# Tridiagonalisation on one core: fewer semaphore waits on the vector engine, and b·u moved behind the mixed row

## The chip, the cores and the metric

The kernel runs on one core of a Trainium2 chip. A core has five engines that each follow an instruction stream of their own: PE (TensorE, matmuls), DVE (VectorE), ACT (ScalarE), POOL (GpSimd) and SP (which only issues transfers here). They share the on-chip memories SBUF and PSUM and meet through semaphores: an instruction can add to one when it completes, and an instruction can be held until one has reached a value. The metric is the device time of one execution in microseconds (us); lower is better.

## The reference

The program computes four graph layers on x of 128 x 64 nodes x 256 features. Only the first part of layer 0 matters here: the eigenvectors of a 64 x 64 matrix that is made from the adjacency.

```python
def _L0_gnn_ref(features, A, W1, b1, W2, b2):
    deg = jnp.sum(A, axis=0) + jnp.sum(A, axis=1) - jnp.diagonal(A)
    d_inv_sqrt = jnp.where(deg > 0, jax.lax.rsqrt(deg), 0.0)
    L = jnp.diag(deg) - A
    L_norm = d_inv_sqrt[:, None] * L * d_inv_sqrt[None, :]
    _, U = jnp.linalg.eigh(L_norm)
    agg = jnp.einsum('mn,bnd->bmd', U.T, features)
    h = jax.nn.relu(agg @ W1 + b1)
    out = h @ W2 + b2
    return jnp.einsum('nm,bmd->bnd', U, out)
...
x = _layernorm(x + _L0_gnn_ref(x, adj, ...), axis=-1)
# layer 1: graph convolutions and LSTMs; layer 2: two wide products with batch norms; layer 3: attention
```

Every later product needs U, so the eigenvector work comes first and nothing of the layers runs beside it.

## The kernel before

`tridiagonalise` turns the symmetric 64 x 64 matrix `sym` into a tridiagonal one by 62 Householder steps (`STEPS = NODES - 2`), and collects the reflections in `qT`. Later stages cut the tridiagonal matrix into leaves, sweep them, merge them, and only then start the layers. Each stage is a block that all engines leave together.

One step i works on row i of the matrix, held on all 64 partitions as `rows[i % 2]`, from column e = i + 1 on. Values of one number per partition are columns of small tensors, `col("name", i)`. On DVE a step is a hand-written sequence, and the order of the calls in the loop at L287 is the order on the engine. The trace shows 28 DVE rows a step; they are, by line number of the kernel before:

- L220, L230, L231, L243: from the norm that ACT made (L339) the sign, its reciprocal and then m, the scale of the reflection. `then_inc(m_ready)` on L243 tells ACT.
- L247, L248, L250, L253: the row's head is corrected, the reciprocals `inv_m` and `inv_head` are taken, and b is made from `inv_m` and from `tail2`, a sum of squares that ACT made (L340).
- L259, L265, L267, L269: the product u·y (two rows in the trace, the second reads the accumulator), then beta, `b_y` (b times the PSUM row `y`, for row i + 1) and `b_beta`.
- L271: `b_u`, from `u_col`, which ACT makes (L350) once m is known. ACT's own line L334 and L183 read it.
- L278, L281: `mixed`, a row from `own` (PSUM), `no_tail` (ACT, L346) and `b_y`, and then `factor`.
- L194, L188: `pu`, and then the next row, which needs `factor` and `mixed`.
- L206, L183, L210, L200, L202, L225, L214, L235: the update of `sym` with the step's two rank-one terms, the next row's norm (L200) and its column (L214).

Beside it PE makes four products a step from `sym`: `y` and `own` (L370, L373) as soon as L235 has written `sym`, `p` and `p_col` (L376, L378) once `u_col` is there, and a fifth for `qT` (L363). ACT makes the norm, `tail2`, `turned` (L334), `no_tail` and `u_col`, in this order. POOL subtracts `turned` from `qT` (L391).

What orders the work on one engine is also written out. DVE instructions that read what an earlier DVE instruction wrote wait for a semaphore of DVE's own. `mark` notes at which count of the current semaphore `chain[0]` a result will be there, and `after(...)` waits for the highest count of the results named. Every eighth step `chain[0]` becomes another semaphore, and at that place DVE waits until the old one has reached its last count. The waits for other engines are `dve.wait_ge(p_ready, i + 1)` and the like. Where more than one wait stands ahead of an instruction, all have to be met before it starts.

Of the kernel before, what the change touches and what calls it, by code (L numbers as in the profile page):

```python
# [121 lines left out]
def tridiagonalise(nc, ctx, t, sym, qT, ps, diag, sub, sup, load):  # L122
# [34 lines left out]
    def col(name, i):  # L157
        return wide[name][:, i:i + 1]

    with nc.Block() as block:  # L160
        @block.vector
        def _(dve):
# [5 lines left out]
            def mark(*made):  # L168


                count[made] = done.n + 1
                return done.one()

            def after(*made):


                dve.wait_ge(chain[0], max(count[m] for m in made))

            def minus_update(i):
                e = i + 1  # L180
                dve.wait_ge(p_ready, i + 1)
                dve.wait_ge(b_u_ready, i + 1)
                stt(minus_S[:, e:], p[i % 2][:, e:], col("b_u", i), sym[:, e:], ALU.mult,  # L183
                    ALU.subtract).then_inc(chain[0], mark("minus_S", i))
# [6 lines left out]
            def pu(i):  # L191
                dve.wait_ge(p_ready, i + 1)
                after(("uy", i))
                stt(col("pu", i), p[i % 2][:, i + 1:i + 2], col("m", i), col("uy", i), ALU.mult,  # L194
                    ALU.add).then_inc(chain[0], mark("pu", i))
# [21 lines left out]
            def signed2(i):  # L217
                dve.wait_ge(norm2_ready, i + 1)
                after(("half_sign", i))
                tt(col("signed2", i), col("norm2", i), col("half_sign", i),  # L220
                   ALU.mult).then_inc(chain[0], mark("signed2", i))
# [15 lines left out]

            def scalars(i):


                head = rows[i % 2][:, i + 1:i + 2]
                after(("signed2", i), ("inv", i), ("signed", i))
                stt(col("m", i), col("signed2", i), col("inv", i), col("signed", i), ALU.mult,  # L243
                    ALU.add).then_inc(m_ready, 1)
                dve.wait_ge(m_ready, i + 1)
                dve.wait_ge(r_col_ready, i + 1)
                tt(head, col("m", i), head, ALU.add).then_inc(chain[0], mark("head", i))  # L247
                dve.reciprocal(col("inv_m", i), col("m", i)).then_inc(chain[0], mark("inv_m", i))  # L248
                after(("head", i))
                dve.reciprocal(col("inv_head", i), head).then_inc(chain[0], mark("inv_head", i))  # L250
                dve.wait_ge(tail2_ready, i + 1)
                after(("inv_m", i))
                stt(col("b", i), col("tail2", i), 0.0, col("inv_m", i), ALU.is_gt,  # L253
                    ALU.mult).then_inc(chain[0], mark("b", i))

            def uy(i):
                r, e = rows[i % 2], i + 1
                dve.wait_ge(y_ready, i + 1)
                ttr(junk[2][:, e:], y[i % 2][:, e:], r[:, e:], 1.0, 0.0, ALU.mult, ALU.add,  # L259
                    col("uy", i)).then_inc(chain[0], mark("uy", i))  # L260

            def betas(i):
                e = i + 1
                after(("b", i), ("inv_head", i))
                tt(col("beta", i), col("b", i), col("inv_head", i), ALU.mult).then_inc(chain[0], mark("beta", i))  # L265
                if e < STEPS:
                    ts(b_y[:, e + 1:], y[i % 2][:, e + 1:], col("b", i), None, ALU.mult).then_inc(chain[0], mark("b_y", i))  # L267
                after(("beta", i))
                tt(col("b_beta", i), col("b", i), col("beta", i), ALU.mult).then_inc(chain[0], mark("b_beta", i))  # L269
                dve.wait_ge(u_ready, i + 1)  # L270
                tt(col("b_u", i), col("u_col", i), col("beta", i), ALU.mult).then_inc(b_u_ready, 1)  # L271

            def mix(i):
                e = i + 1
                dve.wait_ge(own_ready, i + 1)
                dve.wait_ge(no_tail_ready, i + 1)
                after(("b_y", i))
                stt(mixed[:, e + 1:], own[i % 2][:, e + 1:], col("no_tail", i), b_y[:, e + 1:], ALU.mult,  # L278
                    ALU.subtract).then_inc(chain[0], mark("mixed", i))
                after(("uy", i), ("b_beta", i))  # L280
                tt(col("factor", i), col("uy", i), col("b_beta", i), ALU.mult).then_inc(chain[0], mark("factor", i))  # L281
# [5 lines left out]
            for i in range(STEPS):  # L287
# [12 lines left out]
                signed(i)  # L300
                scalars(i)
                uy(i)
                betas(i)
                if i + 1 < STEPS:
                    mix(i)
# [5 lines left out]
            last = STEPS - 1  # L311
            b_pu(last)
# [12 lines left out]
        def _(act):  # L325
# [10 lines left out]
            for i in range(STEPS):  # L336
# [7 lines left out]
                if i + 1 < STEPS:  # L344
                    act.wait_ge(tail2_ready, i + 1)
                    act.activation(col("no_tail", i), col("tail2", i), ACT.Relu, bias=1.0,  # L346
                                   scale=-3e38).then_inc(no_tail_ready, 1)
                act.wait_ge(m_ready, i + 1)
                act.wait_ge(r_col_ready, i + 1)
# [2864 lines left out]
```

## Time and profile before

| | us |
|---|---|
| three runs: lowest, median, highest | 2143.3, 2143.85, 2145.32 |
| the profiled execution: its own time | 2142.91 |
| the profiled execution: first to last instruction (span) | 2141.1 |
| of the span: the tridiagonalisation, from its first y product to its last update | 20.2 to 213.4 |
| of the span: leaves, sweeps and merges | 213.4 to about 450 |
| of the span: the layers | about 450 to 2141.1 |

A row of the time line gives the start, the duration, the engine, the line and the operation. DVE overlaps one instruction with the next: the next one may start before the one ahead has ended, so durations add up to more than the time that passes, and what counts is the distance from start to start. Rows with a shape of 64x1 work on one number per partition. Instructions that only wait aren't among the rows.

### The profile page before, as it was taken

The page shows a single profiled execution, that of the slowest core. Times are in us where ns is not written, and L with a number is a line of the kernel's source. Part 1 is how long each engine was busy: PE and PEld are TensorE (multiplying, and loading weights), DVE is VectorE, ACT ScalarE, POOL GpSimd, SP SyncE. Part 2 cuts the span into 40 slices and gives each one's busy share as a digit, 9 for nine tenths or more (in the row PEclk, how much of TensorE's full clock was granted, in tenths as well). Part 3 has the DMA queues.
Part 4 walks back from the last instruction along what each step waited for, and adds up shares of the span by engine and source line. Part 5 has one row for each costly group of instructions (what it writes and reads, how often), then busy time and mean ns, then how long its engine had stood idle before and what let it go on. Part 6 is the DMA issues. An engine that isn't in the chain of part 4 may idle for free.

```text
span 2141.1 us, 32310 instructions
## 1 busy us (share of the span) xinstructions
PE 1787.1 (83%) x9764; PEld 1536.2 (72%) x9764; DVE 1441.6 (67%) x5778; ACT 857.2 (40%) x1766; POOL 661.5 (31%) x1058
## 2 busy tenths in 40 slices
PE   3455333324999999999999999999999999989998
PEld 2333333313999788888889999988888888768886
DVE  7999999986777556544444444444444677877886
ACT  2333122211443466333333333323323465756664
POOL 0011344412234367432333323333332111651221
PEclk9999766656999999999999999999999999999999
DMA  6000000000111000000000000000010311320111
GB/s 192 2 1 2 1 1 1 1 1 20 60 40 40 30 15 15 15 5 10 10 11 10 10 0 10 20 1 0 0 39 10 148 60 60 101 69 21 40 41 60
DMA packets 44705, 62.72 MB, mean 29 GB/s; under 512 B 13985, under 2 KB 33313, under 8 KB 44449
## 3 DMA queue, kind: packets, MB, share of 16 engines
q1 hardware_dynamic: 43984, 61.08, 8.4%
q8 instruction: 51, 0.84, 0.2%
q14 instruction: 78, 0.63, 0.1%
q10 hardware_dynamic: 592, 0.17, 0.0%
HBM read 36.08 MB, written 25.17 MB: 29 GB/s over the span
## 4 chain that ended last, share of the span: by engine, by line
PE 67%; DVE 5%; ACT 3%; POOL 1%; issue 1%; ACTq 0%; another core or an unknown queue 0%; DVEq 0%; POOLq 0%
PE ps L2164 43%; PE ps L2553 4%; PE ps L2755 2%; PE ps L1688 2%; PE ps L1713 2%; PE ps L2769 2%; PE ps L1674 1%; PE ps L1698 1%; PE ps L2809 1%; PE ps L2803 1%; ACT l_raw L1585 1%; PE ps L1665 1%; DVE j_lnstats L1571 1%; PE ps L2792 1%; DVE x L1562 1%
## 5 line engine op out<-in xcount | busy, mean ns | idle before, releaser
L2295 ACT ACTIVATE l_gates<-ps,biases 128x512 f32<-128x512 f32 (+1 forms) x504 | 289.3, 636 | 490.3 <-remote 475.8
L2164 PE MATMUL ps<-l_nodes_in,l_even 128*128 128x512 f32 x1392 | 321.3, 390 | 2.6 <-DVE x L1562 1.9
L2164 PEld LDWEIGHTS ps<-l_nodes_in,l_even 128*128 128x128 f32 x1392 | 260.7, 188 | 59.2 <-DVE x L1562 2.7
L2164 PE MATMUL ps<-l_nodes_in,kept 128*128 128x336 f32 (+1 forms) x1280 | 298.0, 350 | 2.0 <-ACT l_gates L2295 1.8
L2396 DVE TENSOR_TENSOR l_gates<-l_gates 128x512 f32<-128x512 f32 (+1 forms) x72 | 50.3, 698 | 343.1 <-ACT l_gates L2295 343.1
L2076 POOL CAST l_nodes_in<-big 128x512 fp32r (+3 forms) x142 | 100.5, 737 | 549.3 <-remote 519.6
L2164 PEld LDWEIGHTS ps<-l_nodes_in,kept 128*128 128x128 f32 x1280 | 229.2, 188 | 27.4 <-issue 4.3
L2164 PE MATMUL ps<-l_state,l_even 128*128 128x512 f32 x960 | 223.3, 392 | 0.0
L2164 PEld LDWEIGHTS ps<-l_state,l_even 128*128 128x128 f32 x960 | 180.3, 188 | 39.8
L2079 POOL TENSOR_TENSOR l_nodes_in<-big,l_nodes_in 128x512 fp32r<-128x512 f32 (+1 forms) x142 | 200.5, 1433 | 5.7
L995 PE MATMUL ps<-w,sw_xT 128*128 128x128 f32 x256 | 58.2, 419 | 133.8 <-ACT sw_xT L859 133.8
L995 PEld LDWEIGHTS ps<-w,sw_xT 128*128 128x128 f32 x256 | 54.3, 323 | 138.7 <-ACT sw_xT L859 138.7
L2394 DVE TENSOR_TENSOR l_cell<-l_gates 128x512 f32<-128x512 f32 (+1 forms) x72 | 56.7, 788 | 104.7 <-ACT l_gates L2295 104.1
L2164 PE MATMUL ps<-l_state,kept 128*128 128x336 f32 x512 | 120.3, 316 | 0.0
L2315 ACT ACTIVATE l_gates<-l_cell 128x512 f32<-128x512 f32 (+1 forms) x144 | 84.0, 583 | 75.5 <-DVE l_cell L2406 70.1
L2164 PE MATMUL ps<-l_nodes_in,l_odd 128*128 128x336 f32 x352 | 110.9, 315 | 0.0
L2253 PE MATMUL ps<-l_state,kept 128*128 128x512 f32 x384 | 96.1, 400 | 4.1 <-DVE l_state L2372 3.9
L2413 DVE TENSOR_TENSOR big<-l_gates 128x512 f32 (+2 forms) x72 | 85.6, 1206 | 18.6 <-ACT l_gates L2315 17.5
L370 PE MATMUL ps<-sym,td_c_r_col 64*64 64x64 f32 x124 | 27.5, 324 | 81.0 <-DVE sym L235 80.2
L2553 PE MATMUL ps<-n_h,kept 128*128 128x512 f32 x384 | 91.3, 401 | 3.5 <-POOL n_h L2608 2.4
L2553 PEld LDWEIGHTS ps<-n_h,kept 128*128 128x128 f32 x384 | 74.0, 193 | 20.7 <-POOL n_h L2608 2.9
L2164 PEld LDWEIGHTS ps<-l_state,kept 128*128 128x128 f32 x512 | 88.1, 189 | 0.0
(581 smaller groups left out, 3889.2 us busy)
## 6 DMA issues: line engine op xcount, KB each, us to landing
x<-in_x SPq DMA_DIRECT2D x4, 2048.0 KB, 16.9
residual<-s_x SPq DMA_DIRECT2D x16, 512.0 KB, 2.6
x<-residual SPq DMA_DIRECT2D x16, 512.0 KB, 5.3
normed<-l_raw SPq DMA_DIRECT2D x16, 512.0 KB, 2.6
x<-normed SPq DMA_DIRECT2D x16, 512.0 KB, 3.2
out<-a_y SPq DMA_DIRECT2D x15, 512.0 KB, 2.9
l_raw<-in_L_gnn_W SPq DMA_DIRECT2D x16, 256.0 KB, 2.7
l_raw<-in_L_gnn_W SPq DMA_DIRECT2D x4, 512.0 KB, 3.6
```

Of the source, the lines that this page charges most:

```text
L995: mm = pe.matmul(XW[:, i * HID0:(i + 1) * HID0], xT[:, k, i * TILE:(i + 1) * TILE], w1[:, k, :], start=k == 0, stop=k == KD - 1)
L1688: mm = pe.matmul(G[:, i, :], agg1[:, part, k, i * TILE:(i + 1) * TILE].bitcast(F32R), w["wg0"][:, w_part, k, :].bitcast(F32R), start=part ...
L2076: return eng.tensor_copy(cut.windows(nodes_in[:, slot, HIGH, k, :]).bitcast(F32R), cut.nodes(k, u, step))
L2079: return eng.tensor_tensor(cut.windows(nodes_in[:, slot, LOW, k, :]).bitcast(F32R), cut.nodes(k, u, step), cut.windows(nodes_in[:, slot, H ...
L2164: return pe.matmul(ps[:, 4 * j + gate, 0:n], weight[w_part][:, at:at + 128].bitcast(F32R), src[:, part, k, 0:n].bitcast(F32R), start=start ...
L2253: mm = pe.matmul(F[:, c, :], w["w1"][:, w_part, at:at + 128].bitcast(F32R), agg[:, g % 2, part, k, :].bitcast(F32R), start=k == 0 and w_pa ...
L2295: act.activation(gates[:, j, gate, 0:n], ps[:, 4 * j + gate, 0:n], ACT.Tanh if gate == G else ACT.Sigmoid, bias=bias[:, gate * KD + j:gate ...
L2315: act.activation(gates[:, j, G, 0:n], cell[:, j, 0:n], ACT.Tanh).then_inc(t_ready[j], 1)
L2394: dve.tensor_tensor(cell[:, j, 0:n], gi, gg, ALU.mult).then_inc(c_ready[j], 1)
L2396: dve.tensor_tensor(gi, gi, gg, ALU.mult).then_inc(input_ready[j], 1)
L2413: return dve.tensor_tensor(cut.nodes(j, u, step), cut.windows(go), cut.windows(gt), ALU.mult)
L2553: mm = pe.matmul(O[g % 2][:, j, :], w["w2"][:, w_part, at:at + 128].bitcast(F32R), h[:, g % 2, part, c, :].bitcast(F32R), start=c == 0 and ...
```

## The change

Seven edits in `tridiagonalise`, on DVE unless said otherwise:

1. Waits are dropped where a wait that remains covers them: `p_ready` and `b_u_ready` ahead of `minus_S`, `uy` ahead of `pu`, `norm2_ready` and (but for step 0) `half_sign` ahead of `signed2`, `r_col_ready` ahead of the head's correction, and `tail2_ready` ahead of b.
2. The wait for `no_tail_ready`, which stood ahead of `mixed`, now stands ahead of `inv_m`. ACT makes `no_tail` after `tail2`, so it also stands for `tail2_ready`.
3. The wait for `own_ready`, which stood ahead of `mixed`, now stands ahead of `b_y`.
4. `b_u` moves from ahead of `mixed` to behind it, so that `factor` comes behind `b_u`.
5. `factor` no longer names `uy` in its wait; it waits for `b_beta`, which comes later on the same engine.
6. On ACT the wait for `r_col_ready` ahead of `u_col` is dropped.
7. In the last step ACT also makes `no_tail` and DVE also makes `factor`, neither of which is read; b·pu of the last step waits for that `factor`.

`uy`, `betas` and `mix` are joined into `scalars` and `mix`; the operations and their operands are the same.

```diff
--- before.py
+++ after.py
@@ -178,8 +178,6 @@
 
             def minus_update(i):
                 e = i + 1
-                dve.wait_ge(p_ready, i + 1)
-                dve.wait_ge(b_u_ready, i + 1)
                 stt(minus_S[:, e:], p[i % 2][:, e:], col("b_u", i), sym[:, e:], ALU.mult,
                     ALU.subtract).then_inc(chain[0], mark("minus_S", i))
 
@@ -190,7 +188,6 @@
 
             def pu(i):
                 dve.wait_ge(p_ready, i + 1)
-                after(("uy", i))
                 stt(col("pu", i), p[i % 2][:, i + 1:i + 2], col("m", i), col("uy", i), ALU.mult,
                     ALU.add).then_inc(chain[0], mark("pu", i))
 
@@ -215,8 +212,8 @@
                     col("r_col", i)).then_inc(r_col_ready, 1)
 
             def signed2(i):
-                dve.wait_ge(norm2_ready, i + 1)
-                after(("half_sign", i))
+                if i == 0:
+                    after(("half_sign", i))
                 tt(col("signed2", i), col("norm2", i), col("half_sign", i),
                    ALU.mult).then_inc(chain[0], mark("signed2", i))
 
@@ -235,49 +232,45 @@
                 stt(sym[:, i + 1:], rows[i % 2][:, i + 1:], col("x", i), minus_S[:, i + 1:], ALU.mult,
                     ALU.subtract).then_inc(s_ready, 1)
 
-            def scalars(i):
-
-
-                head = rows[i % 2][:, i + 1:i + 2]
+            def m(i):
                 after(("signed2", i), ("inv", i), ("signed", i))
                 stt(col("m", i), col("signed2", i), col("inv", i), col("signed", i), ALU.mult,
                     ALU.add).then_inc(m_ready, 1)
+
+            def scalars(i):
+
+
+                r, e = rows[i % 2], i + 1
+                head = r[:, e:e + 1]
                 dve.wait_ge(m_ready, i + 1)
-                dve.wait_ge(r_col_ready, i + 1)
                 tt(head, col("m", i), head, ALU.add).then_inc(chain[0], mark("head", i))
+                dve.wait_ge(no_tail_ready, i + 1)
                 dve.reciprocal(col("inv_m", i), col("m", i)).then_inc(chain[0], mark("inv_m", i))
                 after(("head", i))
                 dve.reciprocal(col("inv_head", i), head).then_inc(chain[0], mark("inv_head", i))
-                dve.wait_ge(tail2_ready, i + 1)
                 after(("inv_m", i))
                 stt(col("b", i), col("tail2", i), 0.0, col("inv_m", i), ALU.is_gt,
                     ALU.mult).then_inc(chain[0], mark("b", i))
-
-            def uy(i):
-                r, e = rows[i % 2], i + 1
                 dve.wait_ge(y_ready, i + 1)
                 ttr(junk[2][:, e:], y[i % 2][:, e:], r[:, e:], 1.0, 0.0, ALU.mult, ALU.add,
                     col("uy", i)).then_inc(chain[0], mark("uy", i))
-
-            def betas(i):
-                e = i + 1
                 after(("b", i), ("inv_head", i))
                 tt(col("beta", i), col("b", i), col("inv_head", i), ALU.mult).then_inc(chain[0], mark("beta", i))
+
+            def mix(i):
+                e = i + 1
                 if e < STEPS:
+                    dve.wait_ge(own_ready, i + 1)
                     ts(b_y[:, e + 1:], y[i % 2][:, e + 1:], col("b", i), None, ALU.mult).then_inc(chain[0], mark("b_y", i))
                 after(("beta", i))
                 tt(col("b_beta", i), col("b", i), col("beta", i), ALU.mult).then_inc(chain[0], mark("b_beta", i))
+                if e < STEPS:
+                    after(("b_y", i))
+                    stt(mixed[:, e + 1:], own[i % 2][:, e + 1:], col("no_tail", i), b_y[:, e + 1:], ALU.mult,
+                        ALU.subtract).then_inc(chain[0], mark("mixed", i))
                 dve.wait_ge(u_ready, i + 1)
                 tt(col("b_u", i), col("u_col", i), col("beta", i), ALU.mult).then_inc(b_u_ready, 1)
-
-            def mix(i):
-                e = i + 1
-                dve.wait_ge(own_ready, i + 1)
-                dve.wait_ge(no_tail_ready, i + 1)
-                after(("b_y", i))
-                stt(mixed[:, e + 1:], own[i % 2][:, e + 1:], col("no_tail", i), b_y[:, e + 1:], ALU.mult,
-                    ALU.subtract).then_inc(chain[0], mark("mixed", i))
-                after(("uy", i), ("b_beta", i))
+                after(("b_beta", i))
                 tt(col("factor", i), col("uy", i), col("b_beta", i), ALU.mult).then_inc(chain[0], mark("factor", i))
 
             dve.wait_ge(first_ready, 1)
@@ -298,17 +291,16 @@
                     update(i - 1)
                 signed2(i)
                 signed(i)
+                m(i)
                 scalars(i)
-                uy(i)
-                betas(i)
-                if i + 1 < STEPS:
-                    mix(i)
+                mix(i)
                 if i % SPAN == 0:
                     dve.wait_ge(chain[0], done.n)
                     chain[0], done.n = chains[i // SPAN], 0
                     count = dict.fromkeys(count, 0)
                 pu(i)
             last = STEPS - 1
+            after(("factor", last))
             b_pu(last)
             minus_update(last)
             b_p(last)
@@ -341,12 +333,10 @@
                                accum_out=col("tail2", i)).then_inc(tail2_ready, 1)
                 if i >= 1:
                     turn(i - 1)
-                if i + 1 < STEPS:
-                    act.wait_ge(tail2_ready, i + 1)
-                    act.activation(col("no_tail", i), col("tail2", i), ACT.Relu, bias=1.0,
-                                   scale=-3e38).then_inc(no_tail_ready, 1)
+                act.wait_ge(tail2_ready, i + 1)
+                act.activation(col("no_tail", i), col("tail2", i), ACT.Relu, bias=1.0,
+                               scale=-3e38).then_inc(no_tail_ready, 1)
                 act.wait_ge(m_ready, i + 1)
-                act.wait_ge(r_col_ready, i + 1)
                 act.activation(col("u_col", i), ident[:, e:e + 1], ACT.Identity, bias=col("r_col", i),
                                scale=col("m", i)).then_inc(u_ready, 1)
             turn(STEPS - 1)
```

At the first place, DVE from m to beta in step 1 (`td_m_ready` is set by m, `td_chain0` is DVE's own semaphore, the second ISA row of a line reads the accumulator), the kernel before has

```order
L243 SCALAR_TENSOR_TENSOR td_c_m<-td_c_signed2,td_c_inv,td_c_signed 64x1 [waits td_chain0]
L247 TENSOR_TENSOR td_row1<-td_c_m,td_row1 64x1 [waits td_r_col_ready,td_m_ready]
L248 RECIPROCAL td_c_inv_m<-td_c_m 64x1
L250 RECIPROCAL td_c_inv_head<-td_row1 64x1 [waits td_chain0]
L253 SCALAR_TENSOR_TENSOR td_c_b<-td_c_tail2,td_c_inv_m 64x1 [waits td_chain0,td_tail2_ready]
L259 ISA td_junk2,td_c_uy<-ps,td_row1 64x62 [waits td_y_ready]
L259 ISA td_c_uy 64x1
L265 TENSOR_TENSOR td_c_beta<-td_c_b,td_c_inv_head 64x1 [waits td_chain0]
```

and the changed kernel, at the same place,

```order
L237 SCALAR_TENSOR_TENSOR td_c_m<-td_c_signed2,td_c_inv,td_c_signed 64x1 [waits td_chain0]
L246 TENSOR_TENSOR td_row1<-td_c_m,td_row1 64x1 [waits td_m_ready]
L248 RECIPROCAL td_c_inv_m<-td_c_m 64x1 [waits td_no_tail_ready]
L250 RECIPROCAL td_c_inv_head<-td_row1 64x1 [waits td_chain0]
L252 SCALAR_TENSOR_TENSOR td_c_b<-td_c_tail2,td_c_inv_m 64x1 [waits td_chain0]
L255 ISA td_junk2,td_c_uy<-ps,td_row1 64x62 [waits td_y_ready]
L255 ISA td_c_uy 64x1
L258 TENSOR_TENSOR td_c_beta<-td_c_b,td_c_inv_head 64x1 [waits td_chain0]
```

Nothing moved here; the second waits of the head and of b are gone, and `inv_m` has one.

At the second place, DVE from `b_y` to the update's first term in step 1, the kernel before has

```order
L267 TENSOR_SCALAR td_b_y<-ps,td_c_b 64x61
L269 TENSOR_TENSOR td_c_b_beta<-td_c_b,td_c_beta 64x1 [waits td_chain0]
L271 TENSOR_TENSOR td_c_b_u<-td_c_u_col,td_c_beta 64x1 [waits td_u_ready]
L278 SCALAR_TENSOR_TENSOR td_mixed<-ps,td_c_no_tail,td_b_y 64x61 [waits td_chain0,td_no_tail_ready,td_own_ready]
L281 TENSOR_TENSOR td_c_factor<-td_c_uy,td_c_b_beta 64x1 [waits td_chain0]
L194 SCALAR_TENSOR_TENSOR td_c_pu<-ps,td_c_m,td_c_uy 64x1 [waits td_chain0,td_p_ready]
L188 SCALAR_TENSOR_TENSOR td_row0<-td_row1,td_c_factor,td_mixed 64x61 [waits td_chain0]
L206 TENSOR_TENSOR td_c_b_pu<-td_c_pu,td_c_beta 64x1 [waits td_chain0]
L183 SCALAR_TENSOR_TENSOR td_minus_S<-ps,td_c_b_u,sym 64x62 [waits td_b_u_ready,td_p_ready]
```

and the changed kernel has

```order
L264 TENSOR_SCALAR td_b_y<-ps,td_c_b 64x61 [waits td_own_ready]
L266 TENSOR_TENSOR td_c_b_beta<-td_c_b,td_c_beta 64x1 [waits td_chain0]
L269 SCALAR_TENSOR_TENSOR td_mixed<-ps,td_c_no_tail,td_b_y 64x61 [waits td_chain0]
L272 TENSOR_TENSOR td_c_b_u<-td_c_u_col,td_c_beta 64x1 [waits td_u_ready]
L274 TENSOR_TENSOR td_c_factor<-td_c_uy,td_c_b_beta 64x1 [waits td_chain0]
L191 SCALAR_TENSOR_TENSOR td_c_pu<-ps,td_c_m,td_c_uy 64x1 [waits td_p_ready]
L186 SCALAR_TENSOR_TENSOR td_row0<-td_row1,td_c_factor,td_mixed 64x61 [waits td_chain0]
L203 TENSOR_TENSOR td_c_b_pu<-td_c_pu,td_c_beta 64x1 [waits td_chain0]
L181 SCALAR_TENSOR_TENSOR td_minus_S<-ps,td_c_b_u,sym 64x62
```

`b_u` has moved behind `mixed`, and of the three waits of `mixed`, the two of `pu` and the two of `minus_S` one, one and none are left. A line with a number that the two kernels share, as L248, need not be the same statement.

## Rows read from the trace of the kernel before

**Rows 1.** The page: 40 slices of the span, DVE's busy share and PE's clock in tenths.

```profile
DVE  7999999986777556544444444444444677877886
...
PEclk9999766656999999999999999999999999999999
```

**Rows 2.** Busy time by stretch; columns: stretch, its length, engines, granted clock, DMA.

```profile
20.20:213.40 193.20, 96.25 (x618) 74.72 (x618) 186.01 (x1726) 68.21 (x373) 19.05 (x62) 1.00 0.19 50
...
450.00:520.00 70.00, 25.50 (x82) 13.75 (x82) 51.85 (x307) 6.77 (x19) 9.22 (x7) 0.57 0.00 1
```

**Rows 3.** The instructions of line 370: durations in ns, first and last start.

```profile
L370 PE MATMUL ps<-sym,td_c_r_col x124: 311/323/367, 20.2 to 211.3; 64*64 64x64 f32 x124
```

**Rows 4.** Time line, DVE from m to `minus_S`.

```profile
110.73 0.34 DVE L243 SCALAR_TENSOR_TENSOR td_c_m<-td_c_signed,td_c_inv 64x1 f32<-64x1 f32 x1
...
111.11 0.15 DVE L247 TENSOR_TENSOR td_row<-td_c_m,td_row 64x1 f32<-64x1 f32 x1
...
111.19 0.15 DVE L248 RECIPROCAL td_c_inv_m<-td_c_m 64x1 f32<-64x1 f32 x1
111.29 0.15 DVE L250 RECIPROCAL td_c_inv_head<-td_row 64x1 f32<-64x1 f32 x1
111.44 0.15 DVE L253 SCALAR_TENSOR_TENSOR td_c_b<-td_c_tail,td_c_inv_m 64x1 f32<-64x1 f32 x1
111.52 0.18 DVE L259 CUSTOM_DVE_ANT_0 td_junk<-ps,td_row 64x35 f32<-64x35 f32 x1
...
111.64 0.15 DVE L265 TENSOR_TENSOR td_c_beta<-td_c_b,td_c_inv_head 64x1 f32<-64x1 f32 x1
111.71 0.24 DVE L267 TENSOR_SCALAR td_b_y<-ps,td_c_b 64x34 f32<-64x34 f32 x1
...
111.87 0.14 DVE L269 TENSOR_TENSOR td_c_b_beta<-td_c_b,td_c_beta 64x1 f32<-64x1 f32 x1
...
111.94 0.14 DVE L271 TENSOR_TENSOR td_c_b_u<-td_c_u_col,td_c_beta 64x1 f32<-64x1 f32 x1
...
112.08 0.24 DVE L278 SCALAR_TENSOR_TENSOR td_mixed<-ps,td_c_no_tail,td_b_y 64x34 f32<-64x34 f32 x1
112.25 0.14 DVE L281 TENSOR_TENSOR td_c_factor<-td_c_uy,td_c_b_beta 64x1 f32<-64x1 f32 x1
112.32 0.20 DVE L194 SCALAR_TENSOR_TENSOR td_c_pu<-ps,td_c_m,td_c_uy 64x1 f32<-64x1 f32 x1
112.44 0.24 DVE L188 SCALAR_TENSOR_TENSOR td_row<-td_row,td_c_factor,td_mixed 64x34 f32<-64x34 f32 x1
112.61 0.14 DVE L206 TENSOR_TENSOR td_c_b_pu<-td_c_pu,td_c_beta 64x1 f32<-64x1 f32 x1
112.68 0.24 DVE L183 SCALAR_TENSOR_TENSOR td_minus_S<-ps,td_c_b_u,sym 64x35 f32<-64x35 f32 x1
```

**Rows 5.** The same time line, what ACT, POOL and PE do beside it.

```profile
110.57 0.19 ACT L346 ACTIVATE td_c_no_tail<-td_c_tail 64x1 f32<-64x1 f32 x1
...
110.64 0.44 PE L370 MATMUL ps<-sym,td_c_r_col 64*64 64x64 f32 x2 [1.28 <-DVE sym L235]
...
110.75 0.31 POOL L391 TENSOR_TENSOR eg_qT<-eg_qT,td_turned 64x64 f32<-64x64 f32 x1 [2.77 <-ACT td_turned L334]
...
110.88 0.42 PE L373 MATMUL ps<-sym,tab 64*64 64x64 f32 x2
...
111.11 0.39 ACT L350 ACTIVATE td_c_u_col<-tab,td_c_r_col,td_c_m 64x1 f32<-64x1 f32 x1 [0.35 <-DVE td_c_m L243]
...
111.55 0.47 PE L376 MATMUL ps<-sym,td_c_u_col 64*64 64x64 f32 x2 [0.25 <-ACT td_c_u_col L350]
```

**Rows 6.** Time line, DVE at the place of a longer pause.

```profile
152.14 0.23 DVE L278 SCALAR_TENSOR_TENSOR td_mixed<-ps,td_c_no_tail,td_b_y 64x21 f32<-64x21 f32 x1
152.52 0.15 DVE L281 TENSOR_TENSOR td_c_factor<-td_c_uy,td_c_b_beta 64x1 f32<-64x1 f32 x1 [0.16 <-DVE td_mixed L278]
```

**Rows 7.** DMA queues, 100 to 212 us: packets, MB, share of 16 engines.

```profile
q14 instruction: 13, 0.11, 0.3%
```

## The prediction

> **What bounds the kernel now.** I read the 40 slices first. DVE stands at 9 tenths from the second slice to the eighth, and every later stage needs the eigenvectors, so the first 450 us are one line of work that DVE sets [rows 1]. By stretches, the tridiagonalisation takes 193.2 us and DVE is busy in 186.0 of them; PE's clock is at its full level there (1.00, of 2.4 GHz), so no clock gain hides in it [rows 2]. The first y product starts at 20.2 us and the 62nd at about 211.3, so a step takes 191.1/61 = 3.13 us [rows 3]. Then I read one step on the time line. What counts is the distance from start to start. Two rules come out of it:
>
> - A plain 64x1 instruction is followed by the next start after 0.07 us: `b_beta` to `b_u`, `factor` to `pu` [rows 4]. Such pairs are bound by nothing but DVE's own pace.
> - An instruction that needs a result of one close ahead starts 0.03 to 0.04 us after that one has *ended*: m ends at 110.73 + 0.34 = 111.07 and the head's correction starts at 111.11; that one ends at 111.26 and `inv_head` starts at 111.29 [rows 4].
>
> Two places break the second rule. b needs `inv_m`, which ends at 111.19 + 0.15 = 111.34 (111.33 with the third digit), but b starts at 111.44, 0.11 after it. `mixed` needs `b_y`, which ends at 111.71 + 0.24 = 111.95, but starts at 112.08, 0.13 after it [rows 4]. These two have a second wait, and the result waited for in it was late. Other instructions with two waits lose nothing: `minus_S` starts 0.07 after b·pu, `pu` 0.07 after `factor`, the head 0.04 after m's end [rows 4]; there the second wait had been met long before. The Trainium skill (Perfetto Trace Analysis, Identifying Dependency Chains) says that such an instruction may get EventSemaphore instructions of their own ahead of it. My reading of the rows goes with it: the extra wait holds the instruction stream, and the waiting instruction is only handed to DVE when it is met, 0.07 to 0.09 us later than it would start if it waited at DVE's door.
>
> **The change, part by part.** All waits left are single ones.
>
> *Second wait of b gone.* b can start at 111.33 + 0.04 = 111.37 and at least 0.07 behind `inv_head` (111.36). It was 111.44. Gain 0.07 us a step. What follows must not be late: the u·y product needs y from PE, which ends at 110.64 + 0.44 = 111.08 [rows 5] against a new start of 111.45, 0.37 to spare. `beta` comes behind that product as before.
>
> *`mixed` ahead of `b_u`.* Count from the start of `b_y` at 0. Before: `b_beta` 0.16, `b_u` 0.23, `mixed` 0.37, `factor` 0.54 [rows 4]. After: `b_beta` 0.16, `mixed` when `b_y` has ended, 0.24 + 0.035 = 0.275 (the 0.07 spacing alone would give 0.23), `b_u` 0.17 behind it, 0.445, `factor` 0.07 behind that, 0.515. Gain 0.025 to 0.03 us. So taking the waits off `mixed` is worth 0.09, and 0.07 of that is paid back by `b_u` standing on the path, where before it stood in the shadow of `b_y`. From `factor` on nothing differs: `pu` 0.07 later, the row 0.12 behind `pu` (`factor` has ended 0.14 after its start; 0.14 + 0.035 is less than 0.19), b·pu, `minus_S`.
>
> *Waits moved.* `no_tail` ends at 110.57 + 0.19 = 110.76 and `inv_m` starts at 111.19, 0.43 to spare; `own` ends at 110.88 + 0.42 = 111.30 and the new `b_y` comes at 111.64, 0.34 to spare; p ends at 111.55 + 0.47 = 112.02 and the new `pu` comes at 112.22, 0.20 to spare; `u_col` ends at 111.50 and the new `b_u` comes at 112.08 [rows 4, 5]. Each cost 0 while its cover lasts. Behind each of them the whole rest of the step is queued, so beyond its cover it would cost its full delay 62 times.
>
> *Other waits dropped* (`minus_S`, `pu`, `signed2`, the head, ACT's `u_col`): 0. The first two start at DVE's pace already, `signed2` stands ahead of m, the head follows m's end by 0.04, and `u_col` starts at 111.11 with the head, 0.04 behind m's end [rows 4, 5]. A gain ahead of m would also be lost: m lasts 0.34 where a later instruction of the same kind, `pu`, lasts 0.20, and it ends at 111.07, when POOL's subtraction ends at 110.75 + 0.31 = 111.06 [rows 4, 5]. What holds it is POOL, whose start comes from ACT, and both move with the step. Those 0.13 us stay.
>
> *Fewer instructions in the stream.* Six places of a step had a second wait. Now and then DVE pauses where nothing is late: `factor` starts 0.38 behind `mixed` instead of 0.17 [rows 6]; the instruction queue made 13 fetches in 112 us there [rows 7]. If a wait of its own is an instruction of its own, a step shrinks from 34 to 28, and about a sixth of these pauses goes. With some ten of them at 0.2 to 0.3 us in the stage (an estimate from the one row that stands here) that is 0.4 us; ends 0, if the pauses stay in number, and 2.5, if they are hidden altogether. I take 0.4.
>
> *Last step.* `factor` and `no_tail` are added once: 0.07 us of DVE, the other beside it.
>
> *Sum.* 62 x 0.07 = 4.3 (4.7 with 0.076), 61 x 0.028 = 1.7, 0.4 for the pauses, -0.1 for the last step: 6.3 to 6.8, say 6.7 us. The stage hands all of it on, as nothing later runs beside it. One term is open: the first layers run at a mean clock of 0.57 from 450 to 520 us [rows 2], and the clock's rise needn't come at the same place of the work; 2 us of PE work at the 1.2 GHz level instead of 2.4 is 1 us. I take 0 and keep ±1.5 us, the lower bound being that the rise stays at the same time while the work is 6.7 us ahead, which would cost half of that, 3.3. The profiled execution took 2142.91 us, 0.94 under the median of 2143.85; from the one I get 2136.2, from the other 2137.1. I predict the median, **2137.0 us**.
>
> **The rivals.** *Waits cost nothing (chance 0.10).* b starts exactly when `inv_head` ends (111.44) and `mixed` when `b_u` has ended (112.08) [rows 4]. So both might be held by the instruction just ahead draining, and not by their waits. Then b gains nothing and `mixed`, behind `b_beta`, would start when that ends, 111.87 + 0.14 = 112.01, 0.07 earlier, which `b_u` behind it pays back. Sum 0: 2143.5 us. Against it: `inv_head` itself starts 0.04 before the reciprocal `inv_m` ahead of it ends, and `factor` starts 0.07 before `mixed` ends [rows 4], so neither kind of instruction has to drain. The Trainium skill (VectorE: DVE Perf Modes, The DRAIN you can't avoid) speaks against the change: it tells of eight chained copies that took the same 13.88 us with a semaphore behind each and with one behind the last, and has op count matter, not semaphores. By that rule the sum here is this rival's, 0. Rows at which a single wait costs 0.04 agree with it; those where a second one stands cost 0.11 to 0.13 and don't.
>
> *PE becomes late (0.05).* The cover of `pu` shrinks from 0.30 to 0.20. Ends of PE are modelled; were p 0.25 later than the row says, 0.05 to 0.10 of each step would be lost again: 6.7 - 62 x 0.08 = 1.7 us gain, 2142 us.
>
> *A moved wait stalls (0.03), slower than before.* `no_tail` now guards `inv_m`, 0.9 us earlier in the step than `mixed`. On ACT it stands behind `turned`, which waits for PE and POOL. Its cover is 0.43 us. If it came 0.43 + 0.11 = 0.54 later than the row shows, the gain would be eaten; each further 0.07 costs 62 x 0.07 = 4.3 us, so 0.61 late is 2148 us. For it speaks only that all of ACT's line stands ahead; against it, that `turned` starts by ACT's own order and not after a wait.
>
> *The pauses vanish (0.07).* Without waits that hold the stream, it runs ahead of DVE and covers them: 2.5 instead of 0.4, and 2135 us, or a little less with a lucky clock.
>
> **How the numbers follow.** The forecast (0.75) has the range 2134.5 to 2139.5, from the terms' ends and the clock. The range that holds 8 in 10 adds the rival with the vanished pauses and part of the clock's worst case: 2133.5 to 2140.5. A measurement of this kernel can tell 0.2%, 4.3 us, from no change. Faster by more than that, under 2139.6: the forecast with little of its tail (0.73) and the vanished pauses (0.07), 0.80. Within it: the free waits, PE, and the forecast's tail, 0.17. Slower: 0.03.
>
> **What would show it.** In the changed profile b (L252) starts 0.03 to 0.04 behind the end of `inv_m` (L248), `mixed` (L269) as much behind the end of `b_y` (L264); from `b_y` to `factor` (L274) 0.515 instead of 0.54; m still lasts 0.34; a step is 0.10 shorter and the stage ends near 206.7 instead of 213.4. I am wrong if b still starts at the end of `inv_head`, if `pu` starts with p's end, or if the stage gives 6 us and the layers take them back.

## The result, and the profile after

Six runs of the changed kernel took 2135.1 to 2137.0 us, median 2136.06, against 2143.82 for six of the kernel before. The ratio is 0.9962 with a 95% interval of 0.9949 to 0.9975: 7.8 us, or 0.4%, faster, and clear of no change. The prediction was 2137.0 in a range of 2133.5 to 2140.5. The time came out right; the way to it did not quite, as the stretches show.

The first view is busy time by stretch, columns as in [rows 2]. First the kernel before, cut at the last update of `sym`, at the end of PE's last product in the sweeps, at the first product of layer 0 and at the first LSTM product:

```profile
213.40:435.60 222.20, 79.70 (x392) 74.07 (x392) 214.29 (x1846) 51.44 (x154) 89.56 (x399) 0.66 0.00 1
435.60:504.80 69.20, 14.65 (x49) 6.86 (x48) 55.03 (x362) 5.99 (x21) 4.06 (x18) 0.52 0.00 1
504.80:726.70 221.90, 210.36 (x1377) 187.88 (x1378) 160.18 (x335) 82.22 (x95) 68.83 (x59) 0.97 0.11 44
726.70:2141.10 1414.40, 1383.68 (x7321) 1190.63 (x7319) 818.50 (x1464) 648.14 (x1123) 478.60 (x514) 0.99 0.09 30
```

Then the changed kernel, cut at the same places of the work; its first line answers to the first of [rows 2]:

```profile
20.20:204.30 184.10, 96.26 (x618) 74.72 (x618) 178.78 (x1728) 68.34 (x374) 19.25 (x62) 1.00 0.20 52
204.30:427.60 223.30, 76.06 (x392) 71.33 (x392) 214.18 (x1843) 51.43 (x154) 89.64 (x398) 0.66 0.00 1
427.60:496.90 69.30, 14.62 (x49) 6.86 (x48) 55.30 (x365) 5.99 (x21) 4.35 (x20) 0.55 0.00 1
496.90:721.10 224.20, 213.20 (x1377) 190.03 (x1378) 160.26 (x335) 82.33 (x95) 68.86 (x59) 0.96 0.11 43
721.10:2134.70 1413.60, 1382.24 (x7321) 1189.39 (x7319) 818.62 (x1464) 648.24 (x1123) 478.68 (x514) 0.99 0.09 30
```

The tridiagonalisation became 9.1 us shorter (193.2 to 184.1), not the 6.7 of my sum. The sweeps took 1.1 us more and the stretch from layer 0 to the LSTMs 2.3 us more, the rest 0.8 less. The span fell by 6.4.

The time line of one step, DVE, answers to [rows 4]:

```profile
104.01 0.34 DVE L237 SCALAR_TENSOR_TENSOR td_c_m<-td_c_signed,td_c_inv 64x1 f32<-64x1 f32 x1
...
104.46 0.15 DVE L248 RECIPROCAL td_c_inv_m<-td_c_m 64x1 f32<-64x1 f32 x1
104.57 0.15 DVE L250 RECIPROCAL td_c_inv_head<-td_row 64x1 f32<-64x1 f32 x1
104.65 0.14 DVE L252 SCALAR_TENSOR_TENSOR td_c_b<-td_c_tail,td_c_inv_m 64x1 f32<-64x1 f32 x1
...
104.90 0.24 DVE L264 TENSOR_SCALAR td_b_y<-ps,td_c_b 64x35 f32<-64x35 f32 x1
105.07 0.14 DVE L266 TENSOR_TENSOR td_c_b_beta<-td_c_b,td_c_beta 64x1 f32<-64x1 f32 x1
...
105.18 0.24 DVE L269 SCALAR_TENSOR_TENSOR td_mixed<-ps,td_c_no_tail,td_b_y 64x35 f32<-64x35 f32 x1
...
105.35 0.14 DVE L272 TENSOR_TENSOR td_c_b_u<-td_c_u_col,td_c_beta 64x1 f32<-64x1 f32 x1
105.42 0.15 DVE L274 TENSOR_TENSOR td_c_factor<-td_c_uy,td_c_b_beta 64x1 f32<-64x1 f32 x1
105.48 0.20 DVE L191 SCALAR_TENSOR_TENSOR td_c_pu<-ps,td_c_m,td_c_uy 64x1 f32<-64x1 f32 x1
```

`inv_m` ends at 104.61 and b starts at 104.65; before, b started 0.11 behind it. `b_y` ends at 105.14 and `mixed` starts at 105.18; before it was 0.13. From the start of `b_y` to that of `factor` it is now 0.51 instead of 0.54. m still lasts 0.34. Over all steps the medians went from 0.111 to 0.041 us from the end of `inv_m` to b, and from 0.538 to 0.508 from the start of `b_y` to `factor`.

POOL beside m, and the instruction queue from 100 to 205 us (against 13 fetches in 112 us in [rows 7]):

```profile
104.02 0.31 POOL L381 TENSOR_TENSOR eg_qT<-eg_qT,td_turned 64x64 f32<-64x64 f32 x1 [2.66 <-ACT td_turned L326]
```

```profile
q14 instruction: 11, 0.09, 0.3%
```

### The profile page after: what moved, and what is told of

The parts are those of the page before. It is cut to its first block, busy times and chain, and to the rows that moved or that the text cites. A ratio compares the mean times of both kernels' runs of the same rounds, so it can differ in the third digit from the quotient of the medians.

```text
span 2134.7 us, 31888 instructions
## 1 busy us (share of the span) xinstructions
PE 1784.8 (84%) x9764; PEld 1534.4 (72%) x9764; DVE 1434.7 (67%) x5779; ACT 857.5 (40%) x1767; POOL 662.2 (31%) x1058
## 4 chain that ended last, share of the span: by engine, by line
PE 67%; DVE 5%; ACT 3%; POOL 1%; issue 1%; ACTq 0%; another core or an unknown queue 0%; DVEq 0%; POOLq 0%
PE ps L2154 43%; PE ps L2543 4%; PE ps L1678 2%; PE ps L1703 2%; PE ps L2759 2%; PE ps L2745 2%; PE ps L1664 1%; PE ps L1688 1%; PE ps L1655 1%; PE ps L2799 1%; PE ps L2793 1%; ACT l_raw L1575 1%; DVE j_lnstats L1561 1%; PE ps L2782 1%; DVE x L1552 1%
## 5 line engine op out<-in xcount | busy, mean ns | idle before, releaser
L2154 PE MATMUL ps<-l_state,l_even 128*128 128x512 f32 x960 | 223.3, 392 | 0.0
```

Of the source, the lines that this page charges most:

```text
L2154: return pe.matmul(ps[:, 4 * j + gate, 0:n], weight[w_part][:, at:at + 128].bitcast(F32R), src[:, part, k, 0:n].bitcast(F32R), start=start ...
```

## The experiments

Each was timed at least five times beside the kernel before, on the same chip, and profiled once. "Last update" is the start of the 62nd update of `sym` in the profiled execution: 213.4 us before, 204.3 changed. A *late second wait* is a wait beside another one on the same instruction, for a result that isn't ready yet when the instruction's turn comes; a *met* one has been fulfilled long before. Late second waits here are those of b and `mixed`. The head's correction also waits for two, and one of them, m, is late, but that costs nothing; the next section shows the difference. A *pause* is a DVE row that starts over 0.07 us later behind the row ahead than it does in the steps around it. Not counted is what every kernel has: where DVE changes its semaphore, every eighth step, `pu` waits for `factor` and starts 0.11 later.

**The changed kernel again (`changed_again`).**

> The changed kernel once more, on the same chip as the next three, as their yardstick. Both theories: the last update of the matrix starts near 204.3 us, the time is near 2136, 7 to 8 us under the kernel before.

Measured: 2135.15 us against 2142.88, ratio 0.9965 (0.9952 to 0.9979), last update 204.3. Its stretch from layer 0 to the LSTMs differs from that of the first profile, with the same program:

```profile
20.20:204.30 184.10, 96.26 (x618) 74.72 (x618) 178.78 (x1728) 68.31 (x374) 19.28 (x62) 1.00 0.20 52
...
497.20:719.50 222.30, 210.80 (x1376) 188.18 (x1377) 160.10 (x335) 82.26 (x95) 68.85 (x59) 0.97 0.11 44
719.50:2134.90 1415.40, 1383.89 (x7321) 1190.71 (x7319) 818.41 (x1464) 648.11 (x1123) 478.69 (x514) 0.99 0.09 30
```

The tridiagonalisation takes 184.1 us again; the later stretch took 224.2 us in one execution and 222.3 in the other, at mean granted clocks of 0.96 and 0.97. So the 2.3 us that the first profile "took back" there are for the most part not the change's doing. The whole didn't end sooner for it: the rest took 1415.4 us here and 1413.6 in the first profile, and the spans are 2134.9 and 2134.7.

**b·u put back ahead of the mixed row (`bu_back`).**

```diff
+                dve.wait_ge(u_ready, i + 1)
+                tt(col("b_u", i), col("u_col", i), col("beta", i), ALU.mult).then_inc(b_u_ready, 1)
                 if e < STEPS:
                     after(("b_y", i))
                     stt(mixed[:, e + 1:], own[i % 2][:, e + 1:], ...
-                dve.wait_ge(u_ready, i + 1)
-                tt(col("b_u", i), col("u_col", i), col("beta", i), ALU.mult).then_inc(b_u_ready, 1)
```

> The changed kernel with b u ahead of the mixed row again, as in the kernel before; all waits stay as changed. My theory: the move itself costs, since b u then fills the 0.11 us in which mixed waits for b_y anyway. From the start of b_y, mixed starts at 0.30 instead of 0.275 and factor at 0.47 instead of 0.515, so 0.04 us a step, 61 steps, 2.5 us: the last update starts near 201.8, the time is 2 to 2.5 us under the changed kernel. Rival (the move is what lets the wait go, or mixed is better early): the last update at 204.3 or later, the time the same or up to 2.5 us longer.

Measured: 2132.71 us, ratio 0.9952 (0.9939 to 0.9966), last update 201.1, 2.4 us under the changed kernel on the same chip. The time line of DVE:

```profile
106.40 0.24 DVE L264 TENSOR_SCALAR td_b_y<-ps,td_c_b 64x34 f32<-64x34 f32 x1
106.56 0.14 DVE L266 TENSOR_TENSOR td_c_b_beta<-td_c_b,td_c_beta 64x1 f32<-64x1 f32 x1
106.63 0.15 DVE L268 TENSOR_TENSOR td_c_b_u<-td_c_u_col,td_c_beta 64x1 f32<-64x1 f32 x1
106.70 0.24 DVE L271 SCALAR_TENSOR_TENSOR td_mixed<-ps,td_c_no_tail,td_b_y 64x34 f32<-64x34 f32 x1
106.86 0.14 DVE L274 TENSOR_TENSOR td_c_factor<-td_c_uy,td_c_b_beta 64x1 f32<-64x1 f32 x1
```

`factor` comes 0.46 behind `b_y` instead of 0.51. `mixed` starts 0.03 later, since `b_u` is ahead of it, but `b_u` no longer costs its 0.07 behind it. The move, one of the two things that the change did, costs 3.1 us of the stage.

**The move alone, with all waits of the kernel before (`order_alone`).**

```diff
-                dve.wait_ge(u_ready, i + 1)
-                tt(col("b_u", i), col("u_col", i), col("beta", i), ALU.mult).then_inc(b_u_ready, 1)
...
                 stt(mixed[:, e + 1:], own[i % 2][:, e + 1:], col("no_tail", i), b_y[:, e + 1:], ALU.mult,
                     ALU.subtract).then_inc(chain[0], mark("mixed", i))
+                dve.wait_ge(u_ready, i + 1)
+                tt(col("b_u", i), col("u_col", i), col("beta", i), ALU.mult).then_inc(b_u_ready, 1)
                 after(("uy", i), ("b_beta", i))
```

> The kernel before with b u behind mixed and all its waits kept. Theory: mixed stays at 0.37 behind b_y, since its late wait for b_y decides, and b u now adds its 0.07 to the path: 61 x 0.07 = 4.2 us longer, last update near 217.6, the time near 2147. Rival (mixed is held by b u draining): mixed starts 0.07 sooner, which b u gives back, and the last update stays at 213.4.

Measured: 2148.13 us against 2143.65 on this chip, ratio 1.0019 (1.0010 to 1.0028), last update 217.8:

```profile
113.85 0.24 DVE L267 TENSOR_SCALAR td_b_y<-ps,td_c_b 64x34 f32<-64x34 f32 x1
...
114.22 0.24 DVE L279 SCALAR_TENSOR_TENSOR td_mixed<-ps,td_c_no_tail,td_b_y 64x34 f32<-64x34 f32 x1
114.39 0.14 DVE L282 TENSOR_TENSOR td_c_b_u<-td_c_u_col,td_c_beta 64x1 f32<-64x1 f32 x1
114.45 0.14 DVE L284 TENSOR_TENSOR td_c_factor<-td_c_uy,td_c_b_beta 64x1 f32<-64x1 f32 x1
```

`mixed` starts 0.37 behind `b_y`, as in [rows 4], though `b_u` isn't ahead of it any more. So it was never held by `b_u` draining; the late wait for `b_y` decides. For `mixed`, the rival that waits cost nothing falls with this row; for b it falls with the next run.

**b with one wait (`b_single`).**

```diff
+                dve.wait_ge(tail2_ready, i + 1)
                 dve.reciprocal(col("inv_m", i), col("m", i)).then_inc(chain[0], mark("inv_m", i))
                 after(("head", i))
                 dve.reciprocal(col("inv_head", i), head).then_inc(chain[0], mark("inv_head", i))
-                dve.wait_ge(tail2_ready, i + 1)
                 after(("inv_m", i))
```

> The kernel before with one edit: the wait for tail2 stands ahead of inv_m instead of b, so b has the single wait for inv_m. Theory (a late second wait costs 0.07 to 0.08): b starts 0.04 behind the end of inv_m, 0.075 us a step, 4.6 us: last update near 208.8 instead of 213.4, the time near 2139; mixed is still 0.37 behind b_y. Theory of the pauses: if any late held wait lets them through they stay at 2 to 3 us; if it takes both, they shrink and the last update comes up to 2.5 us sooner. Rival (b is held by the reciprocal ahead of it draining): last update at 213.4.

Measured: 2139.19 us against 2143.65, ratio 0.9981 (0.9972 to 0.9990), last update 208.9:

```profile
109.89 0.15 DVE L251 RECIPROCAL td_c_inv_head<-td_row 64x1 f32<-64x1 f32 x1
109.97 0.14 DVE L253 SCALAR_TENSOR_TENSOR td_c_b<-td_c_tail,td_c_inv_m 64x1 f32<-64x1 f32 x1
...
110.23 0.24 DVE L267 TENSOR_SCALAR td_b_y<-ps,td_c_b 64x34 f32<-64x34 f32 x1
...
110.61 0.24 DVE L278 SCALAR_TENSOR_TENSOR td_mixed<-ps,td_c_no_tail,td_b_y 64x34 f32<-64x34 f32 x1
```

b starts 0.08 behind `inv_head` instead of 0.15. `mixed` is 0.38 to 0.39 behind `b_y`, 0.017 later than before in the median (0.387 against 0.370), which I had not expected and can't explain. Pauses fell from 14 rows with 3.0 us to 10 with 1.8.

**The mixed row with one wait (`mixed_single`).** `no_tail`'s wait ahead of `inv_m`, `own`'s ahead of `b_y`, b with its two waits, b·u ahead of `mixed`.

```diff
+                if i + 1 < STEPS:
+                    dve.wait_ge(no_tail_ready, i + 1)
                 dve.reciprocal(col("inv_m", i), col("m", i)).then_inc(chain[0], mark("inv_m", i))
...
+                    dve.wait_ge(own_ready, i + 1)
                     ts(b_y[:, e + 1:], y[i % 2][:, e + 1:], col("b", i), None, ALU.mult).then_inc(chain[0], mark("b_y", i))
...
-                dve.wait_ge(own_ready, i + 1)
-                dve.wait_ge(no_tail_ready, i + 1)
                 after(("b_y", i))
```

> The kernel before with the waits of mixed alone edited: no_tail ahead of inv_m, own ahead of b_y, mixed has the single wait for b_y; b u stays ahead of it, b keeps two waits. Theory: mixed at 0.30 behind the start of b_y (spacing behind b u) instead of 0.37, 0.07 us a step, 61 steps, 4.3 us: last update near 209.1; b still 0.11 behind the end of inv_m. Pauses as for b_single. Rival (mixed is held by b u draining): last update at 213.4.

Measured: 2140.49 us against 2143.65, ratio 0.9985 (0.9976 to 0.9994), last update 208.4. The time line of DVE:

```profile
110.03 0.24 DVE L270 TENSOR_SCALAR td_b_y<-ps,td_c_b 64x34 f32<-64x34 f32 x1
...
110.26 0.15 DVE L274 TENSOR_TENSOR td_c_b_u<-td_c_u_col,td_c_beta 64x1 f32<-64x1 f32 x1
110.33 0.24 DVE L279 SCALAR_TENSOR_TENSOR td_mixed<-ps,td_c_no_tail,td_b_y 64x34 f32<-64x34 f32 x1
110.49 0.14 DVE L282 TENSOR_TENSOR td_c_factor<-td_c_uy,td_c_b_beta 64x1 f32<-64x1 f32 x1
```

`mixed` is at 0.298 behind `b_y`, `factor` at 0.459, b still 0.111 behind the end of `inv_m` (medians). Pauses: 13 rows with 2.5 us.

**The waits that were always met, put back into the changed kernel (`met_waits_back`), and taken out of the one before (`met_waits_out`).** Put back:

```diff
+                dve.wait_ge(p_ready, i + 1)
+                dve.wait_ge(b_u_ready, i + 1)
                 stt(minus_S[:, e:], p[i % 2][:, e:], col("b_u", i), sym[:, e:], ALU.mult,
...
                 dve.wait_ge(p_ready, i + 1)
+                after(("uy", i))
                 stt(col("pu", i), p[i % 2][:, i + 1:i + 2], col("m", i), col("uy", i), ALU.mult,
...
-                if i == 0:
-                    after(("half_sign", i))
+                dve.wait_ge(norm2_ready, i + 1)
+                after(("half_sign", i))
...
                 dve.wait_ge(m_ready, i + 1)
+                dve.wait_ge(r_col_ready, i + 1)
                 tt(head, col("m", i), head, ALU.add).then_inc(chain[0], mark("head", i))
```

> The changed kernel with four second waits put back that had been met long before in the kernel before: those of minus_S, pu, signed2 and the head; b and mixed keep single waits. Theory that a second wait costs only where it is late: every start-to-start distance as in the changed kernel, and the last update at 204.3. Theory that each is also an instruction in the stream: distances the same, but pauses of 0.2 to 0.35 us come back at the block changes, up to ten of them, and the last update starts up to 2.5 us later, at 205 to 206.8, with 12 or 13 fetches between 100 and 205 us instead of 11.

Measured: 2135.12 us, against 2135.15 of the changed kernel on the same chip; last update 204.4; no pause. Taken out of the kernel before (the same four places and ACT's `u_col`, b and `mixed` left as they were):

> The kernel before without the waits that had always been met: those of minus_S, the second ones of pu, signed2, the head and ACT's u_col. b keeps two waits, mixed three, and the order stays. Theory: no start-to-start distance changes by over 0.01, a step stays at 3.13 but for the pauses. If the pauses come from the number of instructions, they shrink from 13 in the stage to about 11 (30 instead of 34 a step), if from the two late waits, they stay or shrink little: last update between 212.5 and 213.4. If they vanish, 210.6.

Measured: 2143.29 us against 2143.65, ratio 0.9995 (0.9986 to 1.0004), no difference that can be told. b stays 0.111 behind the end of `inv_m`, `factor` 0.537 behind `b_y`. The last update came at 212.3, as pauses fell from 14 rows with 3.0 us to 7 with 1.5, more than either theory had expected. One of them, ahead of `b_y`:

```profile
89.55 0.15 DVE L261 TENSOR_TENSOR td_c_beta<-td_c_b,td_c_inv_head 64x1 f32<-64x1 f32 x1
89.90 0.25 DVE L263 TENSOR_SCALAR td_b_y<-ps,td_c_b 64x41 f32<-64x41 f32 x1 [0.20 <-issue]
```

"issue" says that nothing was waited for that the profile shows; the usual distance is 0.07.

**POOL's subtraction behind m (`pool_behind_m`).** As b·u put back, and:

```diff
                 pool.wait_ge(turned_ready, i + 1)
+                if i + 1 < STEPS:
+                    pool.wait_ge(m_ready, i + 2)
                 pool.tensor_tensor(qT[:, :], qT[:, :], turned[i % 2][:, :], ALU.subtract).then_inc(q_ready, 1)
```

> As bu_back, and POOL's subtraction from qT waits for the m of the running step. Theory that POOL holds m: m lasts 0.20 us instead of 0.34, and unless the next instructions with two SBUF inputs (the head, b) are held in its place, a step is 0.14 shorter, 8.5 us over the stage: last update near 193. If they are held instead, the head lasts up to 0.4 us and the gain is 0 or a loss of up to 0.1 a step (201.8 to 208). Theory that m is long by itself (its operands): m stays at 0.34 and the last update at 201.8.

Measured: 2127.52 us, ratio 0.9930 (0.9916 to 0.9944), last update 195.3:

```profile
103.34 0.21 DVE L237 SCALAR_TENSOR_TENSOR td_c_m<-td_c_signed,td_c_inv 64x1 f32<-64x1 f32 x1
...
103.58 0.15 DVE L246 TENSOR_TENSOR td_row<-td_c_m,td_row 64x1 f32<-64x1 f32 x1
...
103.69 0.31 POOL L383 TENSOR_TENSOR eg_qT<-eg_qT,td_turned 64x64 f32<-64x64 f32 x1 [2.50 <-DVE td_c_m L237]
...
103.85 0.17 DVE L252 SCALAR_TENSOR_TENSOR td_c_b<-td_c_tail,td_c_inv_m 64x1 f32<-64x1 f32 x1
103.94 0.18 DVE L255 CUSTOM_DVE_ANT_0 td_junk<-ps,td_row 64x35 f32<-64x35 f32 x1
```

m takes 0.21 instead of 0.34; only its overlap with POOL was changed. From m to the head the mean distance falls from 0.368 to 0.245, and from b to the u·y product it rises from 0.070 to 0.097, since b, now beside POOL, lasts 0.17 instead of 0.14. That nets 0.1 a step, 5.9 us of the stage, where the theory without a new hold had 8.5. This is the fastest version, 7.6 us under the changed kernel and 15.4 us under the kernel before on the same chip.

| | waits of b, `mixed` | b·u | pauses, us | last update, us | ratio |
|---|---|---|---|---|---|
| before | 2, 3 | ahead | 3.0 | 213.4 | 1 |
| met waits out | 2, 3 | ahead | 1.5 | 212.3 | 0.9995 |
| b single | 1, 3 | ahead | 1.8 | 208.9 | 0.9981 |
| mixed single | 2, 1 | ahead | 2.5 | 208.4 | 0.9985 |
| move alone | 2, 3 | behind | 3.2 | 217.8 | 1.0019 |
| changed | 1, 1 | behind | 0 | 204.3 | 0.9962 |
| changed, met waits back | 1, 1 | behind | 0 | 204.4 | 0.9963 |
| b·u put back | 1, 1 | ahead | 0 | 201.1 | 0.9952 |
| and POOL behind m | 1, 1 | ahead | 0 | 195.3 | 0.9930 |

## Why the prediction was right, and where it was not

*Second wait of b.* Forecast 0.07 us a step, b 0.03 to 0.04 behind the end of `inv_m`. Measured 0.070 and 0.041; 62 x 0.070 is 4.3 us. `b_single` has it with `mixed` left alone: its last update came 4.5 us sooner, of which 4.3 are b's, 1.2 fewer pauses, and -1.0 (61 x 0.017) the later `mixed`. Right.

The reading behind it, that a wait can be an instruction of its own ahead of the one that it guards, shows in the trace, which has rows for such instructions. In the kernel before, the line of the wait for `r_col_ready` (L246, the second that the head's correction names) and the line in `after` (L177) have them, the latter also at b, seen here in the window 111.3 to 111.5 us:

```profile
L246 DVEq EVENT_SEMAPHORE  x62: 21/21/21, 21.0 to 211.2; - x62
...
L177 DVEq EVENT_SEMAPHORE  x1: 21/21/21, 111.4 to 111.4; - x1
```

The lines that name the first wait (L245 for m, L251 for `tail2`) have none; that wait goes with the instruction itself. At b the late wait, for `inv_m`, is the one that stands alone: it starts 0.04 us behind the end of `inv_m`, lasts 0.02, and b starts 0.05 behind it, 0.111 in all. At `mixed` it is 0.04, 0.05 and 0.045, 0.133 in all. At the head it is the other way round: the late wait, for m, is on the instruction, the met one, for `r_col`, stands alone ahead of it, and the head starts 0.04 behind m's end, as with a single wait. The same holds for `pu` where DVE changes its semaphore: in the changed kernel the wait for `p` stands alone there (L190, eight rows) and `pu` starts 0.035 behind the end of `factor`. So two waits with one of them late cost nothing at 62 and 8 places, and what costs is a late wait that stands alone. By this, naming the wait for `inv_m` ahead of that for `tail2` should do what `b_single` does; no run tested that.

*`mixed` ahead of `b_u`.* Forecast `mixed` at 0.275 and `factor` at 0.515, a gain of 0.025 to 0.03. Measured 0.272 and 0.508, a gain of 0.030, 1.8 us. Right. The split into 0.09 won and 0.07 paid back holds when the move comes first: the old waits with the new order have 0.604, 0.066 worse than 0.538, and taking the waits off then wins 0.096. The other way round, `mixed` with one wait and the old order has 0.459, which is 0.079 won, and the move then costs 0.049. The prediction had every number to see that the move was the wrong half of the change (0.30 for `mixed` and 0.47 for `factor` without it) and did not draw the conclusion.

*Waits moved, waits met.* Forecast 0 for both. `met_waits_back` and `met_waits_out` leave the distances as they were, but for the pauses. Here the rule of the Trainium skill (VectorE: DVE Perf Modes, The DRAIN you can't avoid and Rules for kernel authors), that a semaphore costs nothing extra and that op count is to be kept down rather than semaphores, agrees with the runs: 2135.12 us with the met waits and 2135.15 without. For the two late second waits it doesn't: each cost 0.07 to 0.10 us, with the same operations. The rows also leave no room for the rival by which an instruction is held until the one ahead drains (`order_alone`).

*The pauses.* This term was mis-sized. I took 0.4 us, a sixth of them, by the number of instructions, and gave their disappearance a chance of 0.07. They disappeared: no row of the changed kernel has one. The stage's 9.1 us are 4.3 and 1.8 for the two places and 3.0 for this; the pauses of the kernel before add up to as much. And the number of instructions doesn't bring them by itself: with the met second waits back in each step there is still none, while with one late second wait left (`b_single`, `mixed_single`) there are 1.8 and 2.5 us, and with both (`met_waits_out`) 1.5 us, though DVE's stream has only 131 waiting instructions there against 249 in `met_waits_back`. Where late second waits stand, the number does count: with 371 waiting instructions, in the kernel before, there are 3.0 us. The reading that fits all ten profiles is that a late wait that stands alone holds the instruction stream itself, so that it can't run ahead of DVE, and any hitch in it, such as the turn to a newly fetched block, shows as a pause; with single waits the stream is ahead and covers it. The dependence on late second waits is shown. For the block change speaks that after 80 us each pause, in all five kernels that have any, is followed by an instruction fetch 0.6 to 0.9 us later. In the kernel before, `pu` starts 0.39 behind `factor` at 198.0, and of 40 slices of the DMA traffic from 197.9 to 198.9 us one holds the fetch, at 198.7:

```profile
198.01 0.21 DVE L194 SCALAR_TENSOR_TENSOR td_c_pu<-ps,td_c_m,td_c_uy 64x1 f32<-64x1 f32 x1 [0.24 <-DVE td_c_factor L281]
...
GB/s 0 0 0 0 0 0 0 0 0 0 0 0 0 0 0 0 0 0 0 0 0 0 0 0 0 0 0 0 0 0 0 328 0 0 0 0 0 0 0 0
```

The block change was not varied by itself.

*Handing the gain on.* Forecast: all of it, give or take 1.5 us by the clock. Of 9.1 us, 6.4 arrived in the span of the profiled execution and 7.8 in the medians. The stretch from layer 0 to the LSTMs takes about 222 or about 224 us: in the profiles of the kernel before, `met_waits_out`, the changed kernel's second, `bu_back` and `met_waits_back` the first, in the other five the second. The same program showed both. That is the ±1.5 that I kept for the clock. The sweeps took 222.0 to 222.2 us in the four kernels with 309 or more waiting instructions on DVE in the first stage, 222.9 in two with 131 and 249, and 223.3 to 223.7 in the four with 9; this looks like where the code's blocks fall in the sweeps, 1 to 1.5 us, and stays open. So that my total came close to 7.8 is in part luck. The terms add up to 6.3, and to the 6.7 that I took only with 0.076 for b, which measured 0.070; the stage gave 9.1, with 2.6 more than forecast for the pauses; and about 1.3 us of that came back later, as much as the sweeps grew by.

*POOL holds m.* Said in the prediction and forecast to stay; m is 0.34 in both kernels. The last experiment confirms the cause: with POOL behind m, it is 0.21.

## What to carry to other kernels

On a stage made of many tiny dependent instructions, let each instruction have one wait: put the one that is met early on an earlier instruction, so that the late one is the only one left. Where an instruction keeps two, see in the trace which of them has become an instruction of its own; it shouldn't be the late one. Met waits can stay; dropping them is tidying. An instruction that others don't need soon belongs into the time in which its neighbour waits for a result, not behind it, and the same rows that price a wait price such a move: price the two halves of a change apart.

## What the runs showed of the hardware

- Of two waits on a DVE instruction, the trace shows the second one named as an instruction of its own ahead of it (L246, L177), and none for the first. If the one that stands alone is late, it costs 0.07 to 0.10 us; if it has been met, nothing that can be measured, even where the one on the instruction is late (the head starts 0.04 us behind m's end with either one wait or two).
- Late second waits also let pauses of 0.07 to 0.35 us through, 3.0 us in 193; without them there were none, with 9 or with 249 other waiting instructions in the stage. After 80 us each pause is followed by an instruction fetch 0.6 to 0.9 us later.
- A DVE operation with two SBUF inputs and a scalar from SBUF (m) that starts beside POOL's 64 x 64 subtraction ends only with it: 0.34 instead of 0.21 us, and moving POOL by 0.3 us moves the hold to another instruction, where it cost 0.03.
- One program's layers took 222.3 and 224.2 us between the same two points in two executions, so a gain of 2 us in an early stage can be hidden or doubled in a single profile.
